# Expert 0's weights and biases loaded during the last middle steps, into columns of the stored query

## The chip, the cores and the metric

The kernel runs on one core of a Trainium2 chip. The metric is the device time of one execution in microseconds (us), given as the median of several executions. TensorE is called PE in the profile, VectorE DVE, ScalarE ACT, GpSimd POOL and SyncE SP; 16 DMA engines move data between the device memory and the core's own memory (SBUF).

## What is computed

A graph-transformer layer on 12500 tokens of width 256, in float32. Cut to what matters:

```python
xn = layernorm(x)
x = x + gnn(xn, edges) + linear_attention(xn)   # 8 heads; q is elu(..)+1
h = layernorm(x)
idx, prb = argmax(softmax(h @ gate_w + gate_b)), its probability   # 8 experts
pos = rank of the token within its expert; kept = pos < C          # C = 1954
y = relu(h @ w1[idx] + b1[idx]) @ w2[idx] + b2[idx]                # w1 256x1024, w2 1024x256
x = x + nan_to_num(y * prb * kept)
```

## The kernel before

There are three stages, each a block of its own in which every engine runs its own instruction stream; engines meet through semaphores, and no engine goes on to the next stage before all have finished theirs.

Stage 1 computes, in 25 steps of 500 tokens, the query for all tokens (`q_all`, 128 partitions x 2 chunks x 12500 columns, in SBUF) and a table of graph features in device memory. A float32 product is made from three float32r products of high and low halves (`_hi`, `_lo`) all through the kernel.

Stage 2, the middle, takes 25 steps of 500 tokens again (`over_steps`; `NS` is 25). Step s divides and mixes the stored query columns of step s+1 (`q_ksum`, `den_spread`, `q_scaled`, `mix`), adds the graph part, finds each token's expert and slot, and scatters the token's row to `expert_rows` in device memory. POOL works two steps ahead with its gathers: in step s it issues `gather(s+2)` (four indirect DMAs of `gl`, L740, four of `gx`, L744) and then `scatter(s)` (four, L782). On DVE, `att_scores(s)` (L868) waits for the gathered rows of step s, and `rows_of(s)` (L916) waits for the scatter and the output write of step s-2, which read the buffer that it writes. SP writes out step s (500 tokens, two transfers, L40 and L41), then loads indices and x of step s+2. In step 22 it issues the last such load; in steps 23 and 24 it only writes out. When the middle ends, the block closes and `q_all` is given back.

Stage 3 runs 8 experts x 4 tiles (g = 0 to 31) of 496 slots. SP loads tile 0 (`load_x`, 124 partitions, split in 112 and 12), then b1, w1 and w2 of expert 0 (`load_w`, L1215 and L1216, 1 MB each), b2 spread to 124 partitions (L1225, 992 KB), and tiles 1 to 3. All this goes over SP's one DMA queue. ACT and DVE normalize tile 0 (L1374 to L1288), PE transposes it (L1494), ACT and DVE split it in halves (L1295, L1391) and then split w1 (L1272 on ACT, L1363 on DVE, 8 pieces each). For each f of 8 slices of the hidden layer PE makes the first product into `psH` (`first` below, 6 matmuls, L1538), ACT makes `h_hi` and `hf` from it (L1329, L1331), DVE `h_lo` (L1454), and two slices later PE makes the second product into `psY` (`second(f)`, 12 matmuls, L1515). In the very first tile ACT and DVE split slice f of w2 between these (L1277, L1368), and DVE takes the statistics of tile 1 (L1374) after slice 0. DVE's loop begins only after this line pair:

```python
                dve.wait_ge(s_b2_in, 16)
                dve.wait_ge(s_b1_set, 1)
```

although b2 is first read by `with_bias` in the second tile.

Of the kernel before, what the change touches and what calls it, by code (L numbers as in the profile page):

```python
# [10 lines left out]

# [6 lines left out]
ACT = mybir.ActivationFunctionType  # L18
# [5 lines left out]
P = 128  # L24
# [30 lines left out]
def gps_layer(nc, x, src, dst, gnn_w, attn_l, attn_r, wq, wkv, wproj, bproj,  # L55
              gate_w, gate_b, w1, b1, w2, b2, out):
    N, D = x.shape
    H, DH = attn_l.shape
    E, _, F = w1.shape
    QH = 8  # L60
    QD = D // QH
    KC = D // P
# [5 lines left out]
    T3 = 124  # L68
# [23 lines left out]
    def sem_in(stack, name):  # L92
        return stack.enter_context(nc.semaphore(name))
# [12 lines left out]
    with base:  # L106
# [14 lines left out]
        s_act_passed = sem_in(base, "s_act_passed")  # L121
        late = ExitStack()
# [452 lines left out]
        with ExitStack() as ph, nc.Block() as block:  # L575
# [124 lines left out]
            @block.sync  # L700
            def _(sp):
                def idx(t, s):
                    return t[bass.ds(s * TS, TS)].rearrange("(p j) -> p j", j=J)

                def load(s, par):
                    sp.dma_start(isrc[:, par, :], idx(src, s)).then_inc(idx_in[par], 16)
                    sp.dma_start(idst[:, par, :], idx(dst, s)).then_inc(idx_in[par], 16)
                    split_dma(sp, x_sb[:, par, :, :], tok(x, s, D), T, x_in[par])

                load(0, 0)  # L710
                load(1, 1)
                sp.wait_ge(s_c_zero, 1)
                sp.dma_start(bias_a[0:1, 0:D], bproj.rearrange("(a n) -> a n", a=1)).then_inc(s_c_in, 16)
                sp.dma_start(bias_b[1:2, 0:D], bproj.rearrange("(a n) -> a n", a=1)).then_inc(s_c_in, 16)
                sp.dma_start(gate_bc[:, :], gate_b.rearrange("(a e) -> a e", a=1).partition_broadcast(T))\
                  .then_inc(s_c_in, 16)

                def step(s, par, h, ahead):
                    sp.wait_ge(s_x2_ready, 2 * (s + 1))
                    split_dma(sp, tok(out, s, D), xd[:, par, :, 0:D], T, x_out[par])  # L720
                    if ahead == 2:

                        sp.wait_ge(s_xg_done, s + 1)
                        sp.wait_ge(gat[par], 32 * J * (h + 1))
                        load(s + 2, par)

                over_steps(sp, step)
                for par in range(2):
                    n = NS // 2 + (1 - par)
                    sp.wait_ge(x_out[par], 32 * n)  # L730
                    sp.wait_ge(scat[par], 16 * J * n)
# [381 lines left out]
        late.close()  # L1113
        late.close()

        with ExitStack() as ph, nc.Block() as block:  # L1116
            def sb3(name, shape, dt=F32):
                return sb_in(ph, name, shape, dt)

            NG = E * ST  # L1120
            wraw = sb3("wraw", [P, KC * F + NF * D])
# [6 lines left out]
            b1_rows = sb3("b1_rows", [E * NF, P])  # L1128
            b1_sb = sb3("b1_sb", [P, E * NF])
            b2_bc = sb3("b2_bc", [T3, E, D])  # L1130
            xr = sb3("xr", [T3, ST, J, RW])
# [6 lines left out]
            xn3 = sb3("xn3", [T3, J, D])  # L1138
            xt_hi = sb3("xt3_hi", [P, 2, KC, TS3], F32R)
            xt_lo = sb3("xt3_lo", [P, 2, KC, TS3], F32R)  # L1140
            hf = sb3("hf", [P, 4, TS3])
            h_hi = sb3("h_hi", [P, 4, TS3], F32R)
            h_lo = sb3("h_lo", [P, 4, TS3], F32R)
            yb = sb3("yb", [T3, J, D])
            ys = sb3("ys", [T3, J, D])
            top = sb3("top", [T3, J, D])
            bottom = sb3("bottom", [T3, J, D])
            yc = sb3("yc", [T3, J, D])
            fin = sb3("fin", [T3, J, D], I32)
            o_sb = sb3("o_sb", [T3, 2, J, D])  # L1150
# [6 lines left out]
            s_b_in = sem_in(ph, "s_b_in")  # L1157
            s_b2_in = sem_in(ph, "s_b2_in")
# [39 lines left out]

            def over_experts(eng, body):


                body(0, False)
                with eng.Fori(1, E - 1) as e:
                    body(e, False)
                body(E - 1, True)
# [5 lines left out]
            def _(sp):  # L1211
# [6 lines left out]
                def load_x(g, slot):  # L1218
# [4 lines left out]
                sp.dma_start(b1_rows[:, :], b1.rearrange("e (c p) -> (e c) p", p=P)).then_inc(s_b_in, 16)  # L1223
                load_w(0)
                sp.dma_start(b2_bc[:, :, :], b2.rearrange("(a e) d -> a (e d)", a=1).partition_broadcast(T3)  # L1225
                             ).then_inc(s_b2_in, 16)
# [42 lines left out]
            def _(act):  # L1269
                def split_w1(f, n):  # L1270
                    act.wait_ge(s_w_in, 32 * n)
                    act.activation(w1_hi[:, :, f * P:(f + 1) * P], w1_raw[:, :, f * P:(f + 1) * P], ACT.Copy)\  # L1272
                       .then_inc(s_w1hi, 1)

                def split_w2(f, n):
                    act.wait_ge(s_w_in, 32 * n)
                    act.activation(w2_hi[:, f, :], w2_raw[:, f, :], ACT.Copy).then_inc(s_w2hi, 1)  # L1277
# [19 lines left out]
                act.wait_ge(s_eps_set, 1)  # L1297
                root(0)
                normal(0, 0)
                high_t(0, 0)  # L1300
                act.wait_ge(s_b1_t, 1)
                act.activation(b1_sb[:, :], psY[0][0][:, 0:E * NF], ACT.Copy).then_inc(s_b1_set, 1)
                act.wait_ge(s_b1_set, 1)
                for f in range(NF):
                    split_w1(f, 1)
# [52 lines left out]
            def _(dve):  # L1358
# [34 lines left out]

                stats(0, 0, 1)
                scales(0)
                low_t(0, 0)
                for f in range(NF):
                    split_w1(f, 1)
                dve.wait_ge(s_b2_in, 16)
# [87 lines left out]
            def _(pe):  # L1487
# [10 lines left out]
                pe.wait_ge(s_b_in, 16)  # L1498
# [53 lines left out]

# [22 lines left out]
```

## Time and profile before

| | |
|---|---|
| median of 3 executions | 1644.87 us (1641.97 to 1651.89) |
| the profiled execution | 1646.12 us, its span 1644.4 us |
| stage 3 begins in the span | at 863.70 us (its first DMA issue) |
| PE, PEld, DVE, ACT, POOL busy | 86%, 76%, 72%, 47%, 38% |
| mean granted TensorE clock | 0.911 of full speed |

The profiled execution has all its times counted from the first instruction of the span; the 1.72 us beside the span lie outside the first and the last instruction. A busy PE is not PE at its peak: at half the granted clock the same matmul is busy for longer.

### The profile page before, as it was taken

The page shows a single profiled execution, that of the slowest core. Times are in us where ns is not written, and L with a number is a line of the kernel's source. Part 1 is how long each engine was busy: PE and PEld are TensorE (multiplying, and loading weights), DVE is VectorE, ACT ScalarE, POOL GpSimd, SP SyncE. Part 2 cuts the span into 40 slices and gives each one's busy share as a digit, 9 for nine tenths or more (in the row PEclk, how much of TensorE's full clock was granted, in tenths as well). Part 3 has the DMA queues.
Part 4 walks back from the last instruction along what each step waited for, and adds up shares of the span by engine and source line. Part 5 has one row for each costly group of instructions (what it writes and reads, how often), then busy time and mean ns, then how long its engine had stood idle before and what let it go on. Part 6 is the DMA issues. An engine that isn't in the chain of part 4 may idle for free. (4 is left out here: it accounts for less than half of the span.)

```text
span 1644.4 us, 29280 instructions
## 1 busy us (share of the span) xinstructions
PE 1414.5 (86%) x8633; PEld 1252.5 (76%) x8633; DVE 1178.4 (72%) x3066; ACT 766.7 (47%) x1455; POOL 622.2 (38%) x541
## 2 busy tenths in 40 slices
PE   6999999985858766777724999999999999999995
PEld 5999999974646555565524999999999999999995
DVE  5888888864777767777753676677767686767764
ACT  3455555531112111111114676766767676766762
POOL 1111111117787887888860122222122222222213
PEclk8999999996686787777766999999999999999998
DMA  3555555552445554555425212121121312131100
GB/s 108 127 122 120 119 122 130 127 161 59 105 106 123 125 114 107 113 119 121 104 67 127 76 40 72 44 77 47 41 87 50 94 42 77 48 100 50 26 14 18
DMA packets 122639, 145.22 MB, mean 88 GB/s; under 512 B 61546, under 2 KB 97390, under 8 KB 122469
## 3 DMA queue, kind: packets, MB, share of 16 engines
q1 hardware_dynamic: 70897, 89.24, 21.5%
q0 software_dynamic: 51696, 55.42, 14.0%
q8 instruction: 23, 0.38, 0.1%
q14 instruction: 23, 0.19, 0.0%
HBM read 76.42 MB, written 73.36 MB: 91 GB/s over the span
## 5 line engine op out<-in xcount | busy, mean ns | idle before, releaser
L1256 POOL DMA_INDIRECT out<-o_sb,tok_i x128 | 177.7, 1388 | 604.9 <-issue 604.9
L1454 DVE TENSOR_TENSOR h_lo<-hf,h_hi 128x496 fp32r<-128x496 f32 x256 | 172.8, 675 | 214.4 <-PE psY L1515 88.5
L1515 PE MATMUL psY<-w_hi,h_hi 128*124 128x256 f32 x1024 | 290.1, 283 | 7.6 <-DVE w_lo L1368 7.6
L1515 PE MATMUL psY<-w_hi,h_lo 128*124 128x256 f32 x1024 | 287.8, 281 | 0.0
L1515 PE MATMUL psY<-w_lo,h_hi 128*124 128x256 f32 x1024 | 287.2, 280 | 0.0
L1329 ACT ACTIVATE h_hi<-psH,b_sb 128x496 fp32r<-128x496 f32 x256 | 172.7, 674 | 230.0 <-PE psH L1538 219.5
L1515 PEld LDWEIGHTS psY<-w_hi,h_hi 128*124 128x124 f32 x1024 | 189.3, 185 | 16.0 <-issue 8.0
L1515 PEld LDWEIGHTS psY<-w_lo,h_hi 128*124 128x124 f32 x1024 | 189.5, 185 | 8.9
L1515 PEld LDWEIGHTS psY<-w_hi,h_lo 128*124 128x124 f32 x1024 | 189.7, 185 | 0.0
L1071 PE MATMUL psB<-inv_den,spread_at 128*128 128x125 f32 x400 | 84.0, 393 | 114.0 <-DVE inv_den L856 114.0
L1331 ACT ACTIVATE hf<-psH,b_sb 128x496 f32<-128x496 f32 x256 | 170.9, 668 | 0.0
L1071 PEld LDWEIGHTS psB<-inv_den,spread_at 128*128 128x128 f32 x400 | 77.6, 298 | 118.7 <-DVE inv_den L856 66.8
L1538 PE MATMUL psH<-xt_hi,w_hi 128*128 128x496 f32 x512 | 158.8, 391 | 2.9 <-ACT w_hi L1272 2.9
L740 POOL DMA_INDIRECT gl<-alpha_l_table,isrc x100 | 134.6, 1346 | 60.9 <-issue 58.2
L1538 PE MATMUL psH<-xt_hi,w_lo 128*128 128x496 f32 x512 | 157.3, 388 | 0.0
L1538 PE MATMUL psH<-xt_lo,w_hi 128*128 128x496 f32 x512 | 156.6, 387 | 0.0
L1084 PE MATMUL psM<-mix_w,qp 128*125 128x264 f32 x400 | 148.8, 505 | 0.0
L782 POOL DMA_INDIRECT expert_rows<-xd,slots x100 | 123.6, 1236 | 35.3 <-issue 29.9
L744 POOL DMA_INDIRECT gx<-graph_table,idst x100 | 124.1, 1241 | 30.5 <-issue 29.5
L276 POOL TENSOR_SCALAR rstd<-mv 125x4 f32<-125x4 f32 x25 | 5.6, 224 | 284.6 <-DVE mv L357 284.6
L1538 PEld LDWEIGHTS psH<-xt_hi,w_lo 128*128 128x128 f32 x512 | 96.9, 189 | 19.4
L1538 PEld LDWEIGHTS psH<-xt_lo,w_hi 128*128 128x128 f32 x512 | 96.5, 188 | 19.0
(217 smaller groups left out, 3035.1 us busy)
## 6 DMA issues: line engine op xcount, KB each, us to landing
x_sb<-in_x SPq DMA_DIRECT2D x50, 448.0 KB
wraw<-in_L_ffn_w SPq DMA_DIRECT2D x16, 1024.0 KB, 8.2
expert_rows<-empty POOLq DMA_DIRECT2D x31, 520.0 KB, 5.7
xr<-expert_rows SPq DMA_DIRECT2D x32, 455.0 KB
graph_table<-tab_sb SPq DMA_DIRECT2D x25, 511.0 KB
out<-xd SPq DMA_DIRECT2D x25, 448.0 KB
x_sb<-in_x SPq DMA_DIRECT2D x50, 52.0 KB
out<-o_sb,tok_i POOLq DMA_INDIRECT x128, 4.2
```

Source lines behind the costliest of these rows:

```text
L276: nc.gpsimd.tensor_scalar(rstd[:, :], mv[:, :, 1], EPS, None, ALU.add).then_inc(s_var_ready, 1)
L740: pool.indirect_dma_start(out=gl[:, par, j, :], out_offset=None, in_=table_l, in_offset=bass.IndirectOffsetOnAxis(ap=isrc[:, par, j:j + 1] ...
L744: pool.indirect_dma_start(out=gx[:, par, j, :], out_offset=None, in_=table, in_offset=bass.IndirectOffsetOnAxis(ap=idst[:, par, j:j + 1], ...
L782: pool.indirect_dma_start(out=rows, in_=xd[:, par, j, :], in_offset=None, out_offset=bass.IndirectOffsetOnAxis(ap=slots[:, par, j:j + 1], ...
L1071: ins = nc.tensor.matmul(psB[c][:, j * T:(j + 1) * T], spread_at[:, j, c, :], inv_den[:, :], start=j == 0, stop=j == J - 1)
L1084: ins = nc.tensor.matmul(psM[0:T, j, 0:MW], qp[:, kc, j * T:(j + 1) * T], mix_w[:, kc, :], start=False, stop=kc == KC - 1)
L1256: pool.indirect_dma_start(out=out, in_=o_sb[:, par, j, :], in_offset=None, out_offset=bass.IndirectOffsetOnAxis(ap=tok_i[:, par, j:j + 1], ...
L1329: act.activation(h_hi[:, f % 4, :], psH[f % 2][:, 0:TS3], ACT.Relu, bias=b1_sb[:, bass.ds(e * NF + f, 1)]).then_inc(s_hhi_ready, 1)
L1331: act.activation(hf[:, f % 4, :], psH[f % 2][:, 0:TS3], ACT.Relu, bias=b1_sb[:, bass.ds(e * NF + f, 1)]).then_inc(s_hf_ready, 1)
L1454: nc.vector.tensor_tensor(h_lo[:, f % 4, :], hf[:, f % 4, :], h_hi[:, f % 4, :].bitcast(F32), ALU.subtract).then_inc(s_hlo_ready, 1)
L1515: ins = nc.tensor.matmul(psY[par][j // 2][0:T3, (j % 2) * D:(j % 2 + 1) * D], hh[:, f % 4, j * T3:(j + 1) * T3], w[:, f, :], start=f == 0 ...
L1538: ins = nc.tensor.matmul(psH[f % 2][:, 0:TS3], w[:, kc, f * P:(f + 1) * P], xt[:, par, kc, :], start=n == 0, stop=n == 3 * KC - 1)
```

## The change

Expert 0's w1, w2, b2 and b1 are no longer loaded in stage 3. SP issues them in step 22 of the middle, behind that step's load of x, into columns of `q_all`'s chunk 0 which steps 0 to 21 have used up (6272 of 11000 columns). It waits for two semaphores first: the scaled query and the sums of the query of steps 0 to 21. One semaphore, `s_first_in`, counts the four transfers. `q_all` is kept through stage 3, and `wraw`, `b2_bc`, `b1_rows` and most of the other float32 tiles of stage 3 are now parts of it, in the order in which they are carved. In stage 3 the splitting of w1 and the copy of b1 are moved ahead of the normalization of tile 0 on ACT, and the splitting of w1 ahead of the statistics of tile 0 on DVE. DVE waits for `s_first_in` where it waited for `s_b2_in`.

```diff
+                def first_expert():
+                    sp.wait_ge(s_qp_done, KC * (NS - 3))
+                    sp.wait_ge(s_d_mm, NS - 3)
+                    w1_end, w2_end = KC * F, KC * F + NF * D
+                    b2_end, b1_end = w2_end + E * D, w2_end + E * D + P
+                    sp.dma_start(q_all[:, 0, 0:w1_end].rearrange("p (c f) -> p c f", c=KC),
+                                 w1[0:1, :, :].rearrange("a (c p) f -> p (a c) f", p=P)).then_inc(s_first_in, 16)
+                    sp.dma_start(q_all[:, 0, w1_end:w2_end].rearrange("p (c d) -> p c d", c=NF),
+                                 w2[0:1, :, :].rearrange("a (c p) d -> p (a c) d", p=P)).then_inc(s_first_in, 16)
+                    sp.dma_start(q_all[0:T3, 0, w2_end:b2_end].rearrange("p (a n) -> p a n", a=1),
+                                 b2.rearrange("(a e) d -> a (e d)", a=1).partition_broadcast(T3)).then_inc(s_first_in, 16)
+                    sp.dma_start(q_all[0:E * NF, 0, b2_end:b1_end], b1.rearrange("e (c p) -> (e c) p", p=P))\
+                      .then_inc(s_first_in, 16)
...
                         load(s + 2, par)
+                    if ahead == 2 and isinstance(s, int) and s == NS - 3:
+                        first_expert()
...
-        late.close()
-        late.close()
...
+            space = q_all[:, :, :].rearrange("p c n -> p (c n)")
+            used = [0]
+            def carve(parts, *dims):
+                n = math.prod(dims)
+                a = space[0:parts, used[0]:used[0] + n]
+                used[0] += n
...
-            wraw = sb3("wraw", [P, KC * F + NF * D])
+            wraw = carve(P, KC * F + NF * D)
...
+            def loaded(eng, n):
+                if isinstance(n, int) and n == 1:
+                    eng.wait_ge(s_first_in, 64)
+                else:
+                    eng.wait_ge(s_w_in, 32 * (n - 1))
...
                 load_x(0, 0)
-                sp.dma_start(b1_rows[:, :], b1.rearrange("e (c p) -> (e c) p", p=P)).then_inc(s_b_in, 16)
-                load_w(0)
-                sp.dma_start(b2_bc[:, :, :], b2.rearrange("(a e) d -> a (e d)", a=1).partition_broadcast(T3)
-                             ).then_inc(s_b2_in, 16)
                 for g in range(1, ST):
                     load_x(g, g)
...
                 act.wait_ge(s_eps_set, 1)
+                for f in range(NF):
+                    split_w1(f, 1)
+                act.wait_ge(s_b1_t, 1)
+                act.activation(b1_sb[:, :], psY[0][0][:, 0:E * NF], ACT.Copy).then_inc(s_b1_set, 1)
                 root(0)
                 normal(0, 0)
                 high_t(0, 0)
-                act.wait_ge(s_b1_t, 1)
-                act.activation(b1_sb[:, :], psY[0][0][:, 0:E * NF], ACT.Copy).then_inc(s_b1_set, 1)
                 act.wait_ge(s_b1_set, 1)
-                for f in range(NF):
-                    split_w1(f, 1)
...
+                for f in range(NF):
+                    split_w1(f, 1)
                 stats(0, 0, 1)
                 scales(0)
                 low_t(0, 0)
-                for f in range(NF):
-                    split_w1(f, 1)
-                dve.wait_ge(s_b2_in, 16)
+                dve.wait_ge(s_first_in, 64)
                 dve.wait_ge(s_b1_set, 1)
```

## Rows read from the trace of the kernel before

**Rows 1.** The page, part 4: the chain that ended last, by line.

```profile
PE psY L1515 22%; PE psH L1538 21%; PE psX L1494 2%; DMA b_bc<-in_L_ffn_b 2%; POOL out L1256 0%; POOLq L1116 0%; ACT ys L1315 0%; DVE yc L1422 0%; DVE o_sb L1428 0%; DVE yc L1416 0%; DVE fin L1412 0%; DVE yb L1436 0%; DVE h_lo L1454 0%; DVE bottom L1408 0%; SPq L1215 0%
```

**Rows 2.** The page, part 5: form, count, busy, mean ns, idle before, releaser.

```profile
L1515 PE MATMUL psY<-w_hi,h_hi 128*124 128x256 f32 x1024 | 290.1, 283 | 7.6 <-DVE w_lo L1368 7.6
...
L1538 PE MATMUL psH<-xt_hi,w_hi 128*128 128x496 f32 x512 | 158.8, 391 | 2.9 <-ACT w_hi L1272 2.9
```

**Rows 3.** The chain in order of time, 860 to 960: start, us, what.

```profile
866.27 25.43 DMA b_bc<-in_L_ffn_b
```

**Rows 4.** Timeline, 863 to 901, all engines: start, us, engine line op [idle before, releaser].

```profile
866.27 0.56 SPq L1225 DMA_DIRECT2D b_bc<-in_L_ffn_b  x1
...
868.22 1.40 DVE L1374 BATCH_NORM_STATS2 st6c<-xr 124x6 f32<-124x256 f32 x4 [4.39 <-DMA xr<-expert_rows]
...
876.93 1.25 DVE L1391 TENSOR_TENSOR xt_lo<-psX,xt_hi 128x496 fp32r<-128x496 f32 x2 [4.73 <-ACT xt_hi L1295]
...
878.17 2.56 ACT L1272 ACTIVATE w_hi<-wraw 128x256 fp32r<-128x256 f32 x8 [0.67 <-DMA wraw<-in_L_ffn_w]
878.62 2.77 DVE L1363 TENSOR_TENSOR w_lo<-wraw,w_hi 128x256 fp32r<-128x256 f32 x8 [0.43 <-ACT w_hi L1272]
...
879.19 1.17 PE L1538 MATMUL psH<-xt_hi,w_hi 128*128 128x496 f32 x2 [2.91 <-ACT w_hi L1272]
...
882.13 0.68 ACT L1329 ACTIVATE h_hi<-psH,b_sb 128x496 fp32r<-128x496 f32 x1 [1.40 <-PE psH L1538]
...
884.60 0.60 PE L1538 MATMUL psH<-xt_lo,w_hi 128*128 128x496 f32 x2
...
891.72 0.67 DVE L1454 TENSOR_TENSOR h_lo<-hf,h_hi 128x496 fp32r<-128x496 f32 x1 [10.34 <-DMA b_bc<-in_L_ffn_b]
...
892.84 0.55 PE L1515 MATMUL psY<-w_hi,h_hi 128*124 128x256 f32 x1 [7.64 <-DVE w_lo L1368]
892.92 1.41 DVE L1374 BATCH_NORM_STATS2 st6c<-xr 124x6 f32<-124x256 f32 x4 [0.19 <-DMA xr<-expert_rows]
...
895.32 0.41 DVE L1368 TENSOR_TENSOR w_lo<-wraw,w_hi 128x256 fp32r<-128x256 f32 x1
...
897.37 0.28 PE L1515 MATMUL psY<-w_hi,h_hi 128*124 128x256 f32 x1
...
900.14 0.28 PE L1515 MATMUL psY<-w_hi,h_hi 128*124 128x256 f32 x1
```

**Rows 5.** Windows: busy PE, PEld, DVE, ACT, POOL, granted clock, DMA share, GB/s.

```profile
878.00:880.00 2.00, 0.81 (x2) 0.76 (x3) 1.57 (x6) 1.83 (x6) 0.00 (x0) 0.50 1.12 203
...
888.00:890.00 2.00, 0.00 (x0) 0.00 (x0) 0.00 (x0) 0.00 (x0) 0.00 (x0) 0.95 0.25 93
890.00:892.00 2.00, 0.00 (x0) 0.00 (x0) 0.28 (x1) 0.00 (x0) 0.00 (x0) 0.50 0.25 96
...
900.00:910.00 10.00, 10.00 (x71) 9.25 (x70) 4.21 (x9) 7.87 (x16) 0.00 (x0) 1.00 0.00 0
```

**Rows 6.** Timeline of the middle, 809 to 845: SP, POOL and DVE.

```profile
809.77 0.39 SPq L41 DMA_DIRECT2D x_sb<-in_x  x1
...
813.11 1.22 POOL L744 DMA_INDIRECT gx<-graph_table,idst  x1 [0.30 <-issue]
...
817.43 0.17 DVE L868 TENSOR_TENSOR att<-gl,gx 125x16 f32<-125x16 f32 x1 [2.77 <-DMA gx<-graph_table,idst]
...
824.07 1.29 DVE L916 TENSOR_TENSOR xd<-psM,xg 125x512 f32<-125x512 f32 x2 [0.93 <-DMA expert_rows<-xd,slots]
...
833.55 1.21 POOL L744 DMA_INDIRECT gx<-graph_table,idst  x1 [0.30 <-issue]
...
837.58 0.17 DVE L868 TENSOR_TENSOR att<-gl,gx 125x16 f32<-125x16 f32 x1 [3.64 <-DMA gx<-graph_table,idst]
...
844.26 1.29 DVE L916 TENSOR_TENSOR xd<-psM,xg 125x512 f32<-125x512 f32 x2 [0.98 <-DMA expert_rows<-xd,slots]
```

**Rows 7.** The tile `gx`: its 100 gathers, from issue to landing.

```profile
DMA to landing us min/median/max: 4.1/6.3/7.9
```

More of the change, by code:

```diff
@@ L12 @@
+import math
 from contextlib import ExitStack
@@ L121, in gps_layer @@
         s_act_passed = sem_in(base, "s_act_passed")
+        s_first_in = sem_in(base, "s_first_in")
         late = ExitStack()
@@ L1118, in sb3 @@
                 return sb_in(ph, name, shape, dt)
+            space = q_all[:, :, :].rearrange("p c n -> p (c n)")
[4 more added lines that the diff above has]
+                used[0] += n
+                assert used[0] <= KC * N
+                names = "abc"[:len(dims)]
+                if len(dims) == 1:
+                    return a
+                return a.rearrange(f"p ({' '.join(names)}) -> p {' '.join(names)}", **dict(zip(names, dims)))
             NG = E * ST
-            wraw = sb3("wraw", [P, KC * F + NF * D])
+            wraw = carve(P, KC * F + NF * D)
             w1_raw = wraw[:, 0:KC * F].rearrange("p (c f) -> p c f", c=KC)
@@ L1127, in gps_layer @@
             w2_lo = sb3("w2_lo", [P, NF, D], F32R)
-            b1_rows = sb3("b1_rows", [E * NF, P])
+            b2_bc = carve(T3, E, D)
+            b1_rows = carve(E * NF, P)
             b1_sb = sb3("b1_sb", [P, E * NF])
-            b2_bc = sb3("b2_bc", [T3, E, D])
-            xr = sb3("xr", [T3, ST, J, RW])
+            xr = carve(T3, ST, J, RW)
             st6 = sb3("st6c", [T3, J, 6])
@@ L1137, in gps_layer @@
             eps_c = sb3("eps_c", [P, 1])
-            xn3 = sb3("xn3", [T3, J, D])
+            xn3 = carve(T3, J, D)
             xt_hi = sb3("xt3_hi", [P, 2, KC, TS3], F32R)
             xt_lo = sb3("xt3_lo", [P, 2, KC, TS3], F32R)
-            hf = sb3("hf", [P, 4, TS3])
+            hf = carve(P, 4, TS3)
             h_hi = sb3("h_hi", [P, 4, TS3], F32R)
             h_lo = sb3("h_lo", [P, 4, TS3], F32R)
[L1144 to L1148, printed above, removed]
+            yb = carve(T3, J, D)
+            ys = carve(T3, J, D)
+            top = carve(T3, J, D)
+            bottom = carve(T3, J, D)
+            yc = carve(T3, J, D)
             fin = sb3("fin", [T3, J, D], I32)
-            o_sb = sb3("o_sb", [T3, 2, J, D])
+            o_sb = carve(T3, 2, J, D)
             tok_i = sb3("tok_i", [T3, 2, J], I32)
@@ L1155, in gps_layer @@
             psY = [[ps_in(ph, f"psY{p}{c}", [P, 512]) for c in range(J // 2)] for p in range(2)]
-            s_b_in = sem_in(ph, "s_b_in")
-            s_b2_in = sem_in(ph, "s_b2_in")
             s_w_in = sem_in(ph, "s_w_in")
@@ L1270, in split_w1 @@
                 def split_w1(f, n):
-                    act.wait_ge(s_w_in, 32 * n)
+                    loaded(act, n)
                     act.activation(w1_hi[:, :, f * P:(f + 1) * P], w1_raw[:, :, f * P:(f + 1) * P], ACT.Copy)\
@@ L1275, in split_w2 @@
                 def split_w2(f, n):
-                    act.wait_ge(s_w_in, 32 * n)
+                    loaded(act, n)
                     act.activation(w2_hi[:, f, :], w2_raw[:, f, :], ACT.Copy).then_inc(s_w2hi, 1)
@@ L1496, in transposes @@
                     ins.then_inc(s_t_done, 1)
-                pe.wait_ge(s_b_in, 16)
+                pe.wait_ge(s_first_in, 64)
                 nc.tensor.transpose(psY[0][0][:, 0:E * NF], b1_rows[:, :], ident[0:E * NF, 0:E * NF]).then_inc(s_b1_t, 1)
@@ L1551, in _ @@
                     second(E - 1, ST - 1, f)
+        late.close()
 _INS = ["x", "src", "dst", "L0_gnn_weight", "L0_gnn_attn_l", "L0_gnn_attn_r", "L0_mix_Wq", "L0_mix_Wkv",
```

## The prediction, made before the kernel with the change was run

> **What bounds the kernel now.** I read the page's chain first. It ends on PE: the second and first products of stage 3 hold most of its named shares, and one transfer, the spread of b2, holds 2% [rows 1]. The chain in order of time says where: from 866.27 us for 25.43 us everything hangs on b2, until DVE can go on and PE with it [rows 3]. The groups of PE's two products have 7.6 and 2.9 us of idle time in the whole stage, both of them in this start [rows 2], and PE is full at the full clock from 900 on [rows 5]. So a microsecond taken from what precedes 892.84 comes off the end, and one taken from other engines later is worth nothing. Third, the timeline of the start of stage 3 shows two waits. PE's first product waits for the splitting of w1, which waits for w1 (878.17); PE's second product waits 7.64 us for the low half of w2, which DVE makes only after b2 has let it go at 891.72 [rows 4]. Last the middle stage, where the transfers would go: DVE waits there for the gathered rows at 817.43 (2.77 us) and at 837.58 (3.64 us), and shortly for a scatter at 824.07 and 844.26 [rows 6]. From the gather that lands before 837.58 to the end of the middle there is one chain over DVE and the last scatter.
>
> **The start of stage 3, matched event by event.** I move the times of before, and keep the begin of the stage at first.
>
> First product. Without w1's wait PE is held by the low half of tile 0 instead: 876.93 + 1.25 = 878.18 [rows 4]. Tile 0 itself lands first in SP's queue in both kernels (868.22), so I leave it there. The first matmul starts about 0.1 later, at 878.3, instead of 879.19: **-0.9 us**. The splitting of w1, moved ahead, is hidden if it is done before 868.22: from ACT's first piece to DVE's last it took 878.62 + 2.77 - 878.17 = 3.2 us [rows 4]; begun at 863.9, just behind the first issue of the stage, it ends at 867.1, 1.1 before the statistics of tile 0 could begin. Without that cover (tile 0 landing earlier, or ACT starting late) each microsecond over goes to the end. The copy of b1 is one small ACT operation and has the same cover.
>
> The stall. PE had ended its three first products at 884.60 + 0.60 = 885.20 and stood until 892.84: **-7.64 us**, if what is late next is not later than that. What is next: DVE needs `h_hi` and `hf` of slice 0, which ACT begins at 882.13, two operations of 0.68, so 883.5, then 0.67 for `h_lo` and 0.41 for w2's low half: 884.6 on the old times, before 885.2. Next is slice 1: from `h_lo(0)` at 891.72 to the end of `w_lo(1)` at 895.32 + 0.41 are 4.0 us, the statistics of tile 1 among them. From 882.6 on the new times this gives 886.6, and PE wants it at 887.1 (below). It fits by 0.5 us. Tile 1's load stood behind b2 in SP's queue and landed at 892.92 [rows 4]; with 3 MB fewer ahead it is no longer in the way.
>
> The clock. PE works at half clock in 878 to 880, and the granted clock, 0.95 in 888 to 890, was back at 0.50 in 890 to 892 after PE had stood [rows 5]. Hence `second(0)` and the product behind it took 897.37 - 892.84 = 4.53 us where the next pair took 900.14 - 897.37 = 2.77 [rows 4]. Without the stall the clock that rose during the first products is kept: **-1.76 us**. The first rise, with its slow products, stays in both.
>
> Sum of the start: 0.9 + 7.64 + 1.76 = 10.3 us. In absolute terms: first product 878.3, its three slices 6.0 us as before, `second(0)` at 884.3, `second(1)` at 887.1 against 897.37. After that PE has no idle time, and nothing else of the change touches it: the later weight loads, their buffers' release and the order of work are the same, and that tiles lie in `q_all` alters only addresses. I cost that at nothing.
>
> **The middle.** SP issues four more transfers behind the load at 809.77 [rows 6]. In stage 3 b2's issue took 0.56 us [rows 4], so about 2.3 us of SP, which next has to do something at 825 (the output of step 23): hidden. Its two waits are for steps 0 to 21, which DVE and PE have behind them when step 22's outputs are written; what is queued behind the waits is that same output. What costs is the traffic: 2 MB of weights on all engines, and 992 KB of b2 with a DMA share of 0.25 while it ran alone at 93 to 96 GB/s [rows 5], that is on four of the sixteen. It is 124 rows of 8192 B, 31 on each of the four, at 24 GB/s each: 10.6 us there. The trace has no such transfer beside gathers. Bounds: below by zero, since nothing in the middle is removed and no engine gets less to do, so a gain is excluded; above by the spread of landing times of `gx`, 4.1 to 7.9 us [rows 7]. The last gather of step 24 took 837.58 - 833.55 = 4.03, the least of all, so it has at most 3.8 us to lose by traffic seen so far. Delay of the gather of step 23 (last issue 813.11) is covered by DVE's waits of 0.93 and 3.64 behind it. I take **+0.6 us**: with 2 MB gone in some 10 us and b2 in 10.6 us more, the traffic started at 810 is over near 832, before that last gather is issued, and the nearest row with 0.5 MB beside it is step 23's (817.43 - 813.11 = 4.32, or 0.3 above), doubled for what may linger.
>
> The Trainium skill (DMA: Bandwidth & Descriptors, Why a DMA increments its semaphore by 16 and not by 1) has a transfer use the largest number up to 16 that divides its outer size, which for 124 partitions is 4; the share of 0.25 agrees. The change keeps that form and only moves it. Were b2 split in 112 and 12 rows, the same page would give 16 and 12 engines, and no term above would change, as the start no longer waits for it.
>
> **Sum.** -10.3 + 0.6 = -9.7 us on the profiled execution's 1646.12, thus 1636.4. That execution stood 1.25 us above the median of the runs; on 1644.87 the same difference gives **1635.2 us**, 0.6% less. No change and 1% are about what a measurement of this kernel can tell apart.
>
> **Rivals.**
>
> *A: gathers and scatters queue beside b2.* If each of the four engines serves one row of b2 between two indirect rows, an indirect DMA (125 rows, 8 on each engine if evenly spread) needs 8 x 0.34 = 2.7 us there, while POOL issues one each 1.5 us (1.22 + 0.30 [rows 6]). In the 10.6 us of b2 the backlog grows to about 3 of them, 4 to 5 us late. Falling on step 21's scatter (DVE at 824.07), 3.64 of it is covered; falling on step 24's gathers, none is. For it: the four engines hold b2 longest. Against: by my times b2 is through before the last gather. Price: the 3.8 us of the upper bound, 1635.2 - 0.6 + 3.8 = 1638.4. In the Trainium skill (same page, Queues, rings and completion order) each engine takes turns between its queues, a packet at a time; that is this case, and its extent here is open.
>
> *B, the other side: the gather waits for the whole load.* If rows of step 23's gather, issued until 813.11, pass only when SP's queue is empty, they land when b2 does. b2 took 25.43 us in stage 3 with about as much ahead [rows 3]; from 811.8 that is 837.2 instead of 817.43. Of these 19.8 us, 0.93 + 3.64 are covered, 15.2 go to the end: 1644.87 - 10.3 + 15.2 = 1649.8. It decides from 14.9 us of delay on, a landing past 832.3. Against: gathers beside the steps' own loads of 0.5 MB have never landed later than 7.9 us.
>
> *C: the start gives less.* The margins are 1.1 us (w1's splitting before tile 0) and 0.5 us (slice 1 for `second(1)`). If ACT or DVE starts its moved work 3 us late, or the short lead brings small stalls in the first tile, 2 to 3 us are lost: about 1637.5.
>
> *D: the change does not do what it says.* If the waits held SP into step 23, b2 would run until about 847 beside step 24's gathers, and the end of stage 2 be late by A's or more: 1640. What the waits name was finished long before, so I give it little.
>
> **How the numbers follow.** Chances: the forecast 0.62, A 0.18, C 0.11, B 0.04, D 0.03, something else 0.02. Below, the gain can't pass the 10.3 us of the start by much; from the fastest run of before (1641.97), 10.3 less is 1631.7, and I go to 1631. Above, A with D reaches 1640, and single runs of before stray upward by up to 7 us; I stop at 1641.5. Faster by over 1% needs 16 us, which no row holds: 0.04. Slower by over 1% needs B at nearly twice its price: 0.03. The rest, 0.93, is within 1%.
>
> **What the changed profile would show.** `first_expert`'s issues right behind step 22's load of x at about 810, without a wait. DVE's waits for `gx` of step 23 longer than 2.8 us, and that of step 24 within 1 us of 3.6: the first issue of stage 3 then comes within 1 us of 863.7. ACT's and DVE's splitting of w1 done before tile 0's statistics. PE's first product 14.6 us behind the begin of the stage (15.5 before), and `second(0)` 20.6 behind it (29.1 before) with no stall; one rise of the clock instead of two. b2 gone from the chain. The prediction is wrong if the begin of stage 3 moves by more than 4 us, or if PE stands again between the first products and `second(1)`.

## The result, and the profile after

The kernel with the change takes 1639.0 us (median of 13 executions, 1634.55 to 1641.61) against 1647.12 us of the kernel before beside it: ratio 0.9947, 95% interval 0.9935 to 0.9960, so 0.5% faster: 8.1 us between the medians, 8.7 by the ratio. Its profiled execution has a span of 1636.7 us. Run again later (e11 below) it came to 0.9967 (0.9957 to 0.9978), 1642.11 us beside 1648.01 us; the two intervals meet only at their ends, and I take the gain as 5 to 9 us.

The page of the kernel after, the chain by engine and the idle time of the two products: b2's transfer is gone from the chain and the idle time of 7.6 us [rows 2] is gone with it.

```profile
PE 45%; DVE 0%; issue 0%; POOL 0%; POOLq 0%; ACT 0%; ACTq 0%; DVEq 0%
...
L1547 PE MATMUL psY<-w_hi,h_hi 128*124 128x256 f32 x1024 | 289.3, 282 | 0.0
...
L1570 PE MATMUL psH<-xt_hi,w_hi 128*128 128x496 f32 x512 | 158.4, 391 | 2.2 <-issue 2.1
```

The timeline of stage 3's start in the kernel after (columns as in [rows 4]). SP's first row is the begin of the stage.

```profile
868.26 0.36 SPq L41 DMA_DIRECT2D q_all<-expert_rows  x1
...
868.43 2.56 ACT L1304 ACTIVATE w_hi<-q_all 128x256 fp32r<-128x256 f32 x8 [14.41 <-DVE eps_c L1391]
...
871.11 1.28 ACT L1314 ACT_TABLE_LOAD   x1
...
872.77 1.41 DVE L1406 BATCH_NORM_STATS2 st6c<-q_all 124x6 f32<-124x256 f32 x4 [1.13 <-DMA q_all<-expert_rows]
...
874.72 0.30 ACT L1314 ACTIVATE std<-mvc,eps_c 124x4 f32<-124x4 f32 x1 [2.33 <-DVE mvc L1411]
...
881.62 1.17 PE L1570 MATMUL psH<-xt_hi,w_hi 128*128 128x496 f32 x2 [2.12 <-issue]
...
887.48 0.28 PE L1547 MATMUL psY<-w_hi,h_hi 128*124 128x256 f32 x1
...
890.22 0.28 PE L1547 MATMUL psY<-w_hi,h_hi 128*124 128x256 f32 x1
```

From the begin of the stage to the first matmul of `second(1)` it takes 890.22 - 868.26 = 21.96 us; before it was 897.37 - 863.70 = 33.67 [rows 4]. That is 11.71 us less. In pieces, each as a difference to the begin of the stage or to the row ahead: the square root of tile 0's variance comes 6.46 us after the begin, where it was 871.50 - 863.70 = 7.80, because ACT loads its table (1.28 us) at 871.11, ahead of the statistics, and not behind them: 1.34. The first product comes 13.36 us after the begin and not 15.49, 0.79 more than that, since w1 is split. From the first product to `second(0)` it is 5.86 us and not 13.65: 7.79. And `second(0)` with the product behind it takes 2.74 us and not 4.53: 1.79. These rows of the timeline of before were not among [rows 4 to 6]: the last issue of its last scatter, its table load and its square root.

```profile
858.32 1.19 POOL L782 DMA_INDIRECT expert_rows<-xd,slots  x1 [0.30 <-issue]
...
870.21 1.28 ACT L1282 ACT_TABLE_LOAD   x1 [20.74 <-DVE mvc L1379]
...
871.50 0.30 ACT L1282 ACTIVATE std<-mvc,eps_c 124x4 f32<-124x4 f32 x1
```

The windows of the same stretch of the kernel after show the granted clock, which stays up once it is up (columns as in [rows 5]). The first row is from the middle: the share of DMA is still 0.30 there, and in e4 below, the same kernel without b2 in the middle, it falls to 0.12 and 0.07 once the weights are through (830 to 834). I read the 0.30 as b2.

```profile
828.00:830.00 2.00, 0.00 (x0) 0.00 (x0) 1.75 (x3) 0.00 (x0) 1.70 (x2) 1.00 0.30 77
...
884.00:886.00 2.00, 1.95 (x8) 1.27 (x6) 0.08 (x1) 1.45 (x3) 0.00 (x0) 0.82 0.00 0
886.00:888.00 2.00, 1.93 (x11) 1.75 (x12) 2.00 (x6) 1.62 (x4) 0.00 (x0) 1.00 0.00 0
```

Part of this gain was paid back in the middle. The timeline there, SP, POOL and DVE (to be read against [rows 6]):

```profile
811.61 0.40 SPq L42 DMA_DIRECT2D x_sb<-in_x  x1
...
813.22 3.41 SPq L718 DMA_DIRECT2D q_all<-in_L_ffn_b  x1
...
815.13 1.22 POOL L764 DMA_INDIRECT gx<-graph_table,idst  x1 [0.30 <-issue]
...
816.68 2.79 SPq L720 DMA_DIRECT2D q_all<-in_L_ffn_b  x1
...
824.00 0.18 DVE L888 TENSOR_TENSOR att<-gl,gx 125x16 f32<-125x16 f32 x1 [7.15 <-DMA gx<-graph_table,idst]
...
832.40 1.29 DVE L936 TENSOR_TENSOR xd<-psM,xg 125x512 f32<-125x512 f32 x2 [2.61 <-DMA expert_rows<-xd,slots]
...
834.11 1.21 POOL L764 DMA_INDIRECT gx<-graph_table,idst  x1 [0.31 <-issue]
...
843.10 0.18 DVE L888 TENSOR_TENSOR att<-gl,gx 125x16 f32<-125x16 f32 x1 [0.77 <-DMA gx<-graph_table,idst]
```

The load of x of step 24 is issued at 811.61 and not 809.77; up to there the two kernels run the same instructions, and these 1.8 us are drift between two executions. (Over all profiles below, the row stands between 809.77 and 822.93, always ahead of the added transfers.) From that row to the begin of stage 3 it takes 868.26 - 811.61 = 56.65 us, before 863.70 - 809.77 = 53.93. DVE waits 7.15 us for the gathered rows of step 23 (before 2.77), then 2.61 us for step 21's scatter (before 0.93), and the last gather takes 843.10 - 834.11 = 8.99 us to be used (before 4.03). SP stands 3.41 and 2.79 us in the issues of b2 and b1.

### The profile page after: what moved, and what is told of

It is laid out like the page before. It is cut to its first block and busy times, and to the rows that moved or that the text cites. A ratio compares the mean times of both kernels' runs of the same rounds, so it can differ in the third digit from the quotient of the medians.

```text
span 1636.7 us, 29281 instructions
## 1 busy us (share of the span) xinstructions
PE 1411.3 (86%) x8633; PEld 1251.5 (76%) x8633; DVE 1176.4 (72%) x3066; ACT 765.9 (47%) x1455; POOL 621.9 (38%) x541
## 5 line engine op out<-in xcount | busy, mean ns | idle before, releaser
L1288 POOL DMA_INDIRECT out<-q_all,tok_i x128 | 177.5, 1387 | 592.9 <-issue 592.9
L1486 DVE TENSOR_TENSOR h_lo<-q_all,h_hi 128x496 fp32r<-128x496 f32 x256 | 173.0, 676 | 207.9 <-PE psY L1547 88.0
L1091 PE MATMUL psB<-inv_den,spread_at 128*128 128x125 f32 x400 | 88.4, 408 | 125.8 <-DVE inv_den L876 125.8
L1091 PEld LDWEIGHTS psB<-inv_den,spread_at 128*128 128x128 f32 x400 | 81.8, 312 | 130.5 <-DVE inv_den L876 83.3
L1363 ACT ACTIVATE q_all<-psH,b_sb 128x496 f32<-128x496 f32 x256 | 170.7, 667 | 0.0
L802 POOL DMA_INDIRECT expert_rows<-xd,slots x100 | 122.1, 1221 | 40.4 <-issue 31.2
```

Source lines behind the costliest of these rows:

```text
L802: pool.indirect_dma_start(out=rows, in_=xd[:, par, j, :], in_offset=None, out_offset=bass.IndirectOffsetOnAxis(ap=slots[:, par, j:j + 1], ...
L1091: ins = nc.tensor.matmul(psB[c][:, j * T:(j + 1) * T], spread_at[:, j, c, :], inv_den[:, :], start=j == 0, stop=j == J - 1)
L1288: pool.indirect_dma_start(out=out, in_=o_sb[:, par, j, :], in_offset=None, out_offset=bass.IndirectOffsetOnAxis(ap=tok_i[:, par, j:j + 1], ...
L1363: act.activation(hf[:, f % 4, :], psH[f % 2][:, 0:TS3], ACT.Relu, bias=b1_sb[:, bass.ds(e * NF + f, 1)]).then_inc(s_hf_ready, 1)
L1486: nc.vector.tensor_tensor(h_lo[:, f % 4, :], hf[:, f % 4, :], h_hi[:, f % 4, :].bitcast(F32), ALU.subtract).then_inc(s_hlo_ready, 1)
```

## The experiments

Two lengths are read from each run's profile: the *middle*, from the second issue of the last load of x to the first issue of stage 3, and the *start*, from there to the first matmul of `second(1)`.

| kernel | middle | start | ratio to before (95%) |
|---|---|---|---|
| before | 53.93 | 33.67 | 1 |
| after | 56.65 | 21.96 | 0.9947 (0.9935 to 0.9960) |
| e11: after, again | 55.99 | 22.86 | 0.9967 (0.9957 to 0.9978) |
| e1: b2 behind the tiles, nothing in the middle | 54.18 | 24.17 | 0.9942 (0.9922 to 0.9961) |
| e8: only the wait moved | 52.70 | 31.37 | 0.9999 (0.9987 to 1.0011) |
| e5: e1, table and w1 early | 52.09 | 22.93 | 0.9930 (0.9910 to 0.9950) |
| e2: before, four unused transfers | 58.08 | 35.19 | 1.0043 (1.0029 to 1.0057) |
| e7: before, unused b2 | 58.02 | 32.89 | 1.0055 (1.0039 to 1.0072) |
| e9: e7 with b2 split | 53.39 | 34.56 | 1.0012 (0.9999 to 1.0025) |
| e3: after with b2 split | 57.01 | 21.97 | 0.9943 (0.9922 to 0.9963) |
| e4: after, b2 behind the tiles | 54.59 | 22.04 | 0.9935 (0.9915 to 0.9955) |
| e10: after, all four in the last step | 60.17 | 22.73 | 0.9993 (0.9983 to 1.0003) |
| e6: e4, the rest in the last step | 53.17 | 22.06 | 0.9920 (0.9900 to 0.9941) |
| e12: e6 again, beside e11 | 52.42 | 22.12 | 0.9932 (0.9919 to 0.9945) |

The middle of the four kernels that put nothing there (before, e1, e8, e5) is 52.1 to 54.2 us (mean 53.2), which is how well one profile can tell it. The profiled executions of e7, e8 and e9 are the slowest of their runs and late from the start: stage 1 first writes its table at 41.7 to 42.3 us, in the others at 36.9 to 40.4. Why is not known, so of these profiles I use only lengths between rows and not the whole span.

My theory (1) was: the gain is the stall behind b2 and the clock lost in it, with two smaller pieces; the loss is in the middle, where the transfers hold gathers and scatters. The rivals: the early weights carry the gain; the longer middle is drift between executions; of the transfers it is the weights, not b2, that hold the gathers.

**e1, the stall taken away without the middle.**

```diff
-                dve.wait_ge(s_b2_in, 16)
...
                 load_w(0)
-                sp.dma_start(b2_bc[:, :, :], ...).then_inc(s_b2_in, 16)
                 for g in range(1, ST):
                     load_x(g, g)
+                sp.dma_start(b2_bc[:, :, :], ...).then_inc(s_b2_in, 16)
...
                 def with_bias(n, par, e):
+                    if isinstance(n, int) and n == 1:
+                        dve.wait_ge(s_b2_in, 16)
```

> Kernel before, with b2's load issued behind the four tile loads of stage 3 and DVE's wait for it moved to its first use; nothing goes into the middle. Theory 1 (the gain is the stall behind b2 and the second rise of the clock; w1's load is a small part): PE's second product follows the first three without a stall, about 13 us before that of the kernel before is reduced to about 6; 7.6 + 1.8 = 9.4 us less, ratio 0.994, as good as the whole change (0.9947). Rival (the weights' early arrival carries the gain): less than 3 us less, ratio above 0.998, since w1 and w2 still arrive in stage 3.

Its timeline, DVE's splitting of w1 and PE's products:

```profile
882.95 2.76 DVE L1363 TENSOR_TENSOR w_lo<-wraw,w_hi 128x256 fp32r<-128x256 f32 x8
...
883.51 1.17 PE L1538 MATMUL psH<-xt_hi,w_hi 128*128 128x496 f32 x2 [2.39 <-ACT w_hi L1272]
...
890.16 0.28 PE L1515 MATMUL psY<-w_hi,h_hi 128*124 128x256 f32 x1
...
892.93 0.28 PE L1515 MATMUL psY<-w_hi,h_hi 128*124 128x256 f32 x1
```

`second(0)` follows the first product by 6.65 us and `second(1)` by 2.77 more, at the full clock. The start is 9.5 us shorter, the ratio 0.9942: one wait and one load moved within stage 3 give as much as the whole change. The rival that needs the early weights is out. What e1 lacks against the kernel after is 2.2 us of the start: its first product comes 14.75 us after the begin and not 13.36, and `second(0)` 6.65 us behind that and not 5.86. What it saves is the middle.

**e8, the wait alone.** The first and the last hunk of e1, without the new order of loads.

> Kernel before with DVE's wait for b2 moved to its first use, and the order of SP's loads kept, so that the tiles 1 to 3 still stand behind b2. Theory 1 (transfers of SP's queue pass the four engines in order): DVE stands 9 us in the statistics of tile 1 instead, PE's second product starts early but the next waits; 1 to 3 us less, ratio 0.999. Rival (the wait alone was the cost): like e1, 9.4 us less, ratio 0.994.

The timeline, DVE's statistics of tile 1 and PE's `second(1)`:

```profile
897.38 1.40 DVE L1374 BATCH_NORM_STATS2 st6c<-xr 124x6 f32<-124x256 f32 x4 [8.53 <-DMA xr<-expert_rows]
...
900.30 0.54 PE L1515 MATMUL psY<-w_hi,h_hi 128*124 128x256 f32 x1 [7.13 <-DVE w_lo L1368]
```

DVE now stands 8.53 us for tile 1, which was issued behind b2, PE stands 7.13 us one slice later, and the clock falls again (that matmul takes 0.54 us). The start is 2.3 us shorter, but the stretch behind it 2.8 us longer (749.8 us to the end and not 747.0), and the ratio is 1.000. I had expected 1 to 3 us; the stall moves one slice on, nearly whole. So moving the wait is not enough: tile 1, issued behind b2, is still late, and with tile 1 issued ahead of b2 (e1) it is not.

**e5, the other two pieces of the start, also without the middle.** To e1:

```diff
                 act.wait_ge(s_eps_set, 1)
+                act.activation(warm[:, :], eps_c[:, :], ACT.Sqrt)
                 root(0)
...
-                    sp.dma_start(w1_raw, w1e).then_inc(s_w_in, 16)
+                    w1_sem = s_w1_first if isinstance(e, int) and e == 0 else s_w_in
+                    sp.dma_start(w1_raw, w1e).then_inc(w1_sem, 16)
```

> The kernel of e1, and besides w1 of expert 0 waited for alone (its own semaphore) and one small Sqrt on ACT at the begin of stage 3, which loads ACT's table while tile 0 is still on its way. Theory 1 (the start gains 1.3 us by the early table load and 0.9 us by w1; nothing of it needs the middle): from the begin of stage 3 to the second slice's second product 22.4 us, as in the kernel after (21.96), middle as in the kernel before; 11.3 us less, ratio 0.993. Rival (w1's early arrival is needed for the last 2 us): 24.2 us as in e1, ratio 0.9942.

The timeline, ACT's table load, tile 0's square root, the splitting of w1, PE's first product and `second(0)`:

```profile
865.03 1.28 ACT L1304 ACT_TABLE_LOAD   x1 [14.25 <-PEq L575]
...
871.20 0.30 ACT L1288 ACTIVATE std<-mvc,eps_c 124x4 f32<-124x4 f32 x1 [4.67 <-DVE mvc L1386]
...
877.22 1.95 ACT L1278 ACTIVATE w_hi<-wraw 128x256 fp32r<-128x256 f32 x6
...
878.37 1.17 PE L1545 MATMUL psH<-xt_hi,w_hi 128*128 128x496 f32 x2 [2.39 <-ACT w_hi L1278]
...
885.18 0.28 PE L1522 MATMUL psY<-w_hi,h_hi 128*124 128x256 f32 x1
```

The table is loaded at the begin, the square root comes 6.18 us after it (7.58 in e1), so the 1.3 us are the table's. PE waits 2.39 us for the splitting of w1, but ACT splits without a wait for w1 itself, and the first product comes 13.35 us after the begin, as in the kernel after (13.36): nothing is left for an earlier w1 to give. The start is 22.93 us, half a microsecond more than expected and 1 us above the kernel after, and this 1 us lies behind the first product: `second(0)` follows it by 6.81 us and not by 5.86. PE's clock rises later there: counted from the first product, the granted clock of the fourth microsecond is 0.96 in the kernel after and 0.50 in e5, where it is still 0.57 in the sixth. This is not the change's doing, for e11, the same kernel as after, has 0.50 and 0.79 in these places and a start of 22.86 us. So the whole start can be had without the middle. The ratio is 0.993.

**e2, the middle's cost by itself.** The kernel before with `first_expert` as in the change, its four transfers used by nobody; SP waits for them at the end of the middle. This wait costs nothing: stage 3 begins 5.38 us after the last scatter's issue, as in the kernel before.

> Kernel before, with the change's four transfers added in step 22 of the middle, at the same place and into the same columns, but used by nobody (stage 3 loads everything again as before). Theory 1 (the transfers slow the gathers and scatters of steps 21 to 24): DVE waits over 6 us for gx of step 23 instead of 2.8, stage 3 begins about 2.7 us later against step 22's load of x, ratio 1.0015. Rival (the later begin of stage 3 in the changed kernel's one profile was scatter between executions): waits of 2 to 4 us as before, ratio 1.000.

DVE's waits for step 23's gather and step 21's scatter:

```profile
822.63 0.18 DVE L888 TENSOR_TENSOR att<-gl,gx 125x16 f32<-125x16 f32 x1 [7.14 <-DMA gx<-graph_table,idst]
...
832.67 1.29 DVE L936 TENSOR_TENSOR xd<-psM,xg 125x512 f32<-125x512 f32 x2 [4.33 <-DMA expert_rows<-xd,slots]
```

7.14 and 4.33 us: the longer middle is not drift. The middle is 58.08 us, 4.9 above the mean of those with nothing in it, and the ratio 1.0043 is more than my 1.0015.

**e4, the weights without b2.** The kernel after, b2's transfer taken from `first_expert` and put behind the tiles as in e1.

> Kernel after, with only w1, w2 and b1 loaded in the middle; b2 is loaded in stage 3 behind the four tiles and waited for at its first use. Theory 1 (b2 is the culprit in the middle): start of stage 3 as after (about 22 us from its begin to the second slice's second product), middle cost 1 us or less, ratio 0.993. Rival (the weights are the culprit): middle as after, DVE waits 7 us for gx of step 23, ratio 0.9947.

```profile
827.79 0.17 DVE L886 TENSOR_TENSOR att<-gl,gx 125x16 f32<-125x16 f32 x1 [6.80 <-DMA gx<-graph_table,idst]
...
833.42 1.29 DVE L934 TENSOR_TENSOR xd<-psM,xg 125x512 f32<-125x512 f32 x2
...
843.55 0.17 DVE L886 TENSOR_TENSOR att<-gl,gx 125x16 f32<-125x16 f32 x1
```

In these rows DVE waits for the gather of step 23 as long as with b2 (6.80 us), so the weights do hold it, as the rival had it. But then nothing else is held: no wait for the scatter, none for the next gather. DVE's slack takes the delay up, and the middle is 54.59 us, 1.4 above the mean. The ratios of e4 and of the kernel after, 0.9935 and 0.9947, are not told apart by their intervals; the rows are what shows it.

**e7, b2 without the weights.** The kernel before with b2's unused transfer alone, of the same form.

> Kernel before, with b2's transfer alone added in step 22 of the middle, unused. Theory 1 (b2 on four engines holds the scatter of step 21 and the gathers of step 24, the weights hold the gather of step 23, and only both together break through DVE's slack): DVE waits about 3 to 5 us for gx of step 23, 1 to 3 for the scatter behind it, and the begin of stage 3 moves by 1 us or less; ratio 1.000 to 1.001. Rival (b2 alone does it): 57 to 58 us from the last load of x to stage 3 instead of 53.9, ratio 1.002 or more.

```profile
828.18 1.19 POOL L796 DMA_INDIRECT expert_rows<-xd,slots  x1 [0.30 <-issue]
...
831.18 0.24 DVE L882 TENSOR_TENSOR att<-gl,gx 125x16 f32<-125x16 f32 x1 [4.02 <-DMA gx<-graph_table,idst]
...
845.36 1.29 DVE L930 TENSOR_TENSOR xd<-psM,xg 125x512 f32<-125x512 f32 x2 [8.37 <-DMA expert_rows<-xd,slots]
```

Here my theory fell in its size: I had thought that only both together break through. In these rows DVE waits only 4.02 us for step 23's gather, but 8.37 us for step 21's scatter, which nothing covers. From the scatter's last issue to the use it takes 845.36 - 828.18 = 17.2 us, in the kernel before 824.07 - 819.20 = 4.9. The middle is 58.02 us and the ratio 1.0055: 1 MB alone costs as much as all 3 MB. Of the 9 us the profile's middle holds 4.8; where the rest lies is open, the more so as this profile was late before the added transfer was issued.

**e9, the same 992 KB on all engines.**

```diff
-                    sp.dma_start(q_all[0:T3, 0, w2_end:b2_end]..., b2...partition_broadcast(T3)).then_inc(s_first_in, 16)
+                    split_dma(sp, q_all[0:T3, 0, w2_end:b2_end]..., b2...partition_broadcast(T3), T3, s_first_in)
```

> The kernel of e7 (before, with b2 alone added in step 22 of the middle, unused) with that transfer split in 112 and 12 partitions, so the same 992 KB go over all engines. Theory 1 (e7's 8.4 us at step 21's scatter are rows that stood beside b2 on its four engines): DVE's waits are those of the kernel before (3 us for gx of step 23, about 1 for the scatter), 54 us from the last load of x to stage 3, ratio 1.000. Rival (1 MB more at this place costs that, however it is spread): 58 us, ratio 1.005.

```profile
831.74 0.18 DVE L882 TENSOR_TENSOR att<-gl,gx 125x16 f32<-125x16 f32 x1 [7.09 <-DMA gx<-graph_table,idst]
...
837.38 1.29 DVE L930 TENSOR_TENSOR xd<-psM,xg 125x512 f32<-125x512 f32 x2
...
847.35 0.17 DVE L882 TENSOR_TENSOR att<-gl,gx 125x16 f32<-125x16 f32 x1
```

The scatter is no longer waited for, and nothing behind it. DVE waits 7.09 us for the gather, against my expectation of 3, and the slack takes it up. The gather itself is no later than in e7: from its last issue to its use it takes 9.3 us here and 9.1 there (4.3 in the kernel before), only POOL had issued it 4 us sooner in e7's profile. The scatter is what differs: used at most 8.8 us after its last issue (828.54), against 17.2. The middle is 53.39 us and the ratio 1.0012 with 1 inside its interval. The kernels of e7 and e9 differ only in the split, and their ratios' intervals lie apart; so it is the form on four engines that holds the scatter, while the gather is held by the 1 MB either way.

**e3, the split in the kernel after.** The same hunk on the kernel after.

> Kernel after, with b2's transfer split in 112 and 12 partitions. Theory 1 (b2 on four engines is what holds the gathers and scatters): the DMA share no longer sits at 0.3 after the weights are in, SP's issues of b2 and b1 take under 1 us instead of 3.4 and 2.8, DVE's waits for gx of steps 23 and 24 fall back towards 3 us; 2 to 2.7 us less than after, ratio to before 0.993. Rival (the 2 MB of weights on all engines are what holds them): as after, 0.9947 within 0.1%, waits of 7 us for step 23.

The middle stays long (57.01 us), SP stands 3.56 us in the issue of b2's first part, and DVE waits 6.54 us for the gather and 2.42 us for the scatter. The rival is right here: with 2 MB of weights ahead, the split saves nothing. The windows fit a split b2 that ends too late as well: the share of DMA stays at 0.92 or more until 832.00, 17.6 us behind the load of x, while in e9 it is down to 0.16 at 13 to 15 us behind it. Spreading helps b2 alone, but not at the end of 3 MB.

**e6, the weights in the last step.** The kernel of e4 with the call moved:

```diff
-                    if ahead == 2 and isinstance(s, int) and s == NS - 3:
+                    if ahead == 0:
                         first_expert()
```

> The kernel of e4 (w1, w2 and b1 in the middle, b2 behind the tiles in stage 3), with the three issues moved from step 22 to the last step, behind its output, when all gathers have landed. Theory 1 (the weights cost by what they do to gathers): DVE's wait for gx of step 23 is back at 3 us, the middle costs nothing, unless the last scatter queues behind the weights; from the last load of x to the begin of stage 3 about 54 us, ratio 0.993. Rival (the last scatter lands later beside 2 MB): 56 us or more, ratio 0.9945.

DVE waits 2.66 us for the gather of step 23, the middle is 53.17 us and the ratio 0.9920, so the weights cost nothing there, and the last scatter, issued up to 862.02, lands as before (stage 3 begins 5.37 us later).

**e10, the same move for all four transfers**, on the kernel after.

> Kernel after with nothing changed but the place: all four issues behind the output of the last step instead of behind step 22's load. Theory 1 (b2's four engines hold whatever comes then: the last scatter and tile 0): the begin of stage 3 or tile 0's statistics 3 to 8 us later than in e6, ratio 0.995 to 0.998. Rival (the place is all, the split of engines nothing): as e6, ratio 0.992.

Its timeline: the issue of w1, the last scatter's last issue, and the begin of stage 3.

```profile
847.07 0.76 SPq L714 DMA_DIRECT2D q_all<-in_L_ffn_w  x1
...
858.20 1.20 POOL L802 DMA_INDIRECT expert_rows<-xd,slots  x1 [0.30 <-issue]
872.88 0.34 SPq L41 DMA_DIRECT2D q_all<-expert_rows  x1
```

From the last scatter's issue to stage 3 it takes 14.7 us, in the kernel before 863.70 - 858.32 = 5.4: with b2 in this place the very last rows land 9.3 us later, more than the 3 to 8 us that I had expected. The middle is 60.17 us, and the whole gain is gone (0.9993). In e6, with b2 left out of this place, the same distance is 5.37 us, so the place alone doesn't do it; which transfer goes there does. That it is b2's form on four engines I take over from e7 and e9; a split b2 in this place was not run.

**e11 and e12, the kernel after and e6 side by side.**

> Kernel after, unchanged, on the same chip as e12. All theories: ratio 0.9947, as measured. For the middle: if its cost is real and not scatter between executions, DVE again waits over 5 us for gx of step 23, and 56 to 58 us lie between the last load of x and stage 3.

> The kernel of e6 again, beside e11: w1, w2 and b1 behind the last output, b2 behind the tiles. Theory 1: 2.5 to 3 us less than e11, ratio 0.992 to 0.993 to the kernel before. Rival (e6 was luck, the middle's cost does not matter): same as e11, 0.9947.

e12's timeline, DVE's two waits, the issue of w1, the begin of stage 3:

```profile
819.81 0.18 DVE L886 TENSOR_TENSOR att<-gl,gx 125x16 f32<-125x16 f32 x1 [2.71 <-DMA gx<-graph_table,idst]
...
838.79 0.17 DVE L886 TENSOR_TENSOR att<-gl,gx 125x16 f32<-125x16 f32 x1 [3.46 <-DMA gx<-graph_table,idst]
...
847.40 0.84 SPq L714 DMA_DIRECT2D q_all<-in_L_ffn_w  x1
...
863.96 0.34 SPq L41 DMA_DIRECT2D q_all<-expert_rows  x1
```

The gather waits are those of the kernel before, stage 3 begins with all weights in place, and the middle is as short as with nothing in it. On the same chip e12's median is 1635.95 us (5 runs) and e11's 1642.11 (8 runs), 6.2 us or 0.4% less and twice what I had expected (their middles and starts differ by 4.3); e6's ratio was 0.9920, e12's 0.9932. This version beats both kernels. It does not beat e5, which puts nothing into the middle and has 0.9930 (0.9910 to 0.9950): by these runs the move of the weights, at its best, gives no more than reordering stage 3. e11 shows the kernel after again with 6.61 and 2.50 us of waits and a middle of 55.99 us.

## Why the prediction was right, and where it was off

The forecast was 9.7 us less; measured were 8.7 (0.53% of 1647.12), and 5.4 in e11. The time of 1639.0 us lies inside the range of 1631 to 1641.5; e11's 1642.11 lies 0.6 above it, on a chip where the kernel before took 1648.01. The forecast's mechanism holds for the start, but that its sum was near is partly luck: two terms were off in opposite ways. The start gained 1.4 us more than forecast (11.7 in the profile, 10.3 forecast), and the middle cost some 2 us more.

*The stall, 7.64 us:* measured 7.79. It fitted by the slack that I had worked out: DVE's `w_lo(1)` was ready and PE did not stand. *The clock, 1.76:* measured 1.79. *The first product, 0.9:* measured 0.79, but this is the value of one execution. It is there because w1 came 0.67 us after ACT was ready for it (878.17 in [rows 4]); with the same load of w1 ACT did not wait for it in e1, e2, e7 and e8, where the first product came 14.60 to 14.90 us after the begin and not 15.49, and waited 1.74 us in e9 (16.52). e1 shows the stall and the clock without the rest, e8 that tile 1 must also stand ahead of b2 for either to be kept.

*A term that I left out, 1.3 us.* I kept tile 0's path at its old times ("Tile 0 itself lands first in SP's queue in both kernels (868.22), so I leave it there"). It lands as before, but ACT's table load of 1.28 us stood on that path, behind the statistics, and with the moved work ahead of it, it comes before them. e5 shows it alone. The table load is a row of the old trace that I had passed over. The Trainium skill (ScalarE: Activation LUTs, What ACT_TABLE_LOAD costs) gives 1283 ns for one; the rows agree with 1.28 us.

*The middle, 0.6 us:* measured 2.7 and 2.1 against the 53.93 of the kernel before, 3.4 and 2.8 against the mean of 53.2 (56.65 in the kernel after, 55.99 in e11). This is the term that was mis-sized. The step that failed is the bound on how late a gather comes, from [rows 7]: gathers beside 0.5 MB had landed within 7.9 us, but the last ones of the kernel after took 8.9 and 9.0 us (824.00 - 815.13, 843.10 - 834.11), since 3 MB is outside what those rows had seen. I also had b2 through by 832, and the last gather, issued at 834.11, was still held. And I bounded only the gathers: the scatter of step 21, used 11.2 us after its last issue (832.40 - 821.19) and not 4.9, had no term in the sum, only in rival A. The covers of 0.93 and 3.64 us worked as I had put them: step 23's output came 6.5 us late (833.72 and not 825.38, less 1.8 of drift), and stage 3 2.7 us late.

*Rival A* (turns beside b2 on four engines) is what happened in kind: e7 against e9 isolates the four engines. Its price, 1638.4 or 6.5 us less, lies between the two measured gains, and the forecast's 9.7 above both. The delay fell on step 21's scatter and on both gathers, the gathers by the weights as well (e4). That it is a matter of turns, row by row, is argued, not shown, and the size speaks against the turns as I had priced them: 4 to 5 us late, where e7's scatter took 12.3 us more than before. What the Trainium skill says of turns by packet (DMA: Bandwidth & Descriptors, Queues, rings and completion order) no run here resolves. *Rival B* did not come: the gathers landed past their time by 4 to 5 us, not 20. *Rival C* lost its chance with the fit of both margins: the splitting of w1 was done before the statistics, with 1.13 us of DVE's idle time left. *Rival D* is out: the issues follow the load of x directly.

*The signs I had named.* That "the begin of stage 3 moves by more than 4 us" did come, if it is read on the span: 868.26 and not 863.70, 4.6 us. Of these 1.8 had gone by before the added transfers were issued, and 2.7 are the middle's. I should have set this sign against the load of x and not against the span, for drift alone can reach it. The first issue of stage 3 was not within 1 us either, and DVE's wait for the last gather was 0.77 us, not within 1 us of 3.6. The other signs came as named: no stall between the first products and `second(1)`, one rise of the clock, b2 gone from the chain; the first product came 13.36 us behind the begin (14.6 forecast) and `second(0)` 19.22 (20.6).

## What to carry to other kernels

Before a load is moved into an earlier stage, look whether anything needs it as early as the wait says, and what else stands behind it in the same queue: here one wait, the place of one load in the queue and an early table load gave as much as the best version of the move. If a load is moved, put it behind the last gather that the old stage waits for: 2 MB of weights cost nothing there, although the last scatter was still to come. A transfer that uses few of the engines is the one to keep away from short indirect transfers, even when its bytes are the smaller part; spreading it over all engines cured it when it came alone, and not behind 2 MB of others.

## What the runs showed of the hardware, unexpected

- SP can stand in an issue behind others: in step 22 the issue behind two of 1 MB took 3.0 to 3.6 us, be it 992 KB (3.41) or only 32 KB (3.39 in e4), and the two ahead of it 0.4 to 0.6; b2 alone (e7) was issued in 0.25. It is not the two of 1 MB alone: in the last step the same issue took 1.7 to 2.2 us (e6, e10, e12), and in stage 3 of the kernel before 0.56. What decides it is open.
- 992 KB on four engines cost the middle 4.6 us more than the same 992 KB on all (e7 and e9), one profile each; what DVE stood for was a scatter used 17.2 us after its last issue.
- The stall in front of a matmul also costs behind it: where PE had stood 6.7 to 9.0 us (before, e2, e7, e8, e9), `second` and the product behind it took 4.5 to 5.2 us, and 2.7 to 2.8 where it had not.
- The granted clock does not rise at the same place in two executions of one kernel: from the first product to `second(0)` the kernel after took 5.86 us in one and 6.59 us in the other (e11).
